# Top-2 expert routing in a two-layer kernel: how the threshold, the slots and the token lists are computed

## The reference

```python
def _L1_ffn_ref(x, router_w, wg, wu, wd):
    E, K, CF = 8, 2, 1.25
    xf = x.reshape(-1, D)                      # N = 4096 tokens
    capacity = max(1, int(CF * N / E))         # 640
    probs = jax.nn.softmax(xf @ router_w.T, axis=-1)
    topw, topi = jax.lax.top_k(probs, K)
    topw = topw / (topw.sum(-1, keepdims=True) + 1e-06)
    fe, fw, ft = topi.reshape(-1), topw.reshape(-1), jnp.repeat(jnp.arange(N), K)
    order = jnp.lexsort((-fw, fe))             # by expert, heaviest first
    se, sw, st = fe[order], fw[order], ft[order]
    rank = jnp.arange(N * K) - starts[se]
    keep = rank < capacity                     # an expert keeps its 640 heaviest
    disp = ...                                 # the kept tokens, [E, 640, D]
    eo = (silu(disp @ wg) * (disp @ wu)) @ wd  # per expert
    out = zeros.at[st].add(eo[...] * (sw * keep)[:, None])
```

## Time and profile before

| | us |
|---|---|
| median of 3 runs | 3220.86 (3217.69 to 3222.49) |
| the profiled execution | 3225.83 |
| its span, from the first instruction to the last | 3224.0 |

### The profile page before, as it was taken

How to read it: one execution, slowest core, us unless ns; L and a number is a source line. 1 busy time by engine, 2 the same in 40 slices (tenths; PEclk the granted TensorE clock), 3 DMA queues, 4 the chain that set the end, 5 groups by cost and what they waited for, 6 DMA issues and landing times. The chain is left out here.

```text
span 3224.0 us, 46683 instructions
## 1 busy us (share of the span) xinstructions
PE 2902.0 (90%) x16106; PEld 1942.3 (60%) x16106; DVE 2127.2 (66%) x4522; ACT 1732.5 (54%) x3308; POOL 1750.2 (54%) x1540
## 2 busy tenths in 40 slices
PE   7999999999999999979954859999999999999176
PEld 6995555565555556558843845656656566565075
DVE  5667777777777777646766336677676766766642
ACT  5666767777676776756731424444444444443032
POOL 0006988889898888831102825454454544444066
PEclk9999999999999999989976979999999999999578
DMA  2004434343343433300011444444444444432034
GB/s 95 1 21 99 100 80 100 82 98 87 90 94 89 93 87 86 74 30 15 21 63 39 78 96 99 102 102 93 112 92 97 102 102 102 104 88 60 26 77 77
DMA packets 182988, 254.00 MB, mean 79 GB/s; under 512 B 35904, under 2 KB 75584, under 8 KB 182208
## 3 DMA queue, kind: packets, MB, share of 16 engines
q1 hardware_dynamic: 168672, 240.19, 31.6%
q0 software_dynamic: 14080, 10.82, 2.5%
HBM read 33.44 MB, written 16.67 MB: 16 GB/s over the span
## 5 line engine op out<-in xcount | busy, mean ns | idle before, releaser
L1766 POOL TENSOR_TENSOR arena<-arena 128x512 f32<-128x512 f32 x1152 | 1444.8, 1283 | 719.6 <-ACT arena L1137 695.8
L794 PE MATMUL psum<-stack 96*128 96x512 f32 (+4 forms) x4096 | 1240.9, 433 | 31.3 <-ACT arena L1137 11.5
L1137 ACT ACTIVATE arena<-psum 128x512 f32<-128x512 f32 x1536 | 854.5, 598 | 507.0 <-PE psum L794 471.0
L1396 DVE TENSOR_REDUCE top<-psum 128x1 f32<-128x512 f32 x1536 | 978.2, 676 | 137.5 <-PE psum L794 130.7
L794 PEld LDWEIGHTS psum<-stack 96*128 96x128 f32 (+4 forms) x4096 | 715.2, 191 | 428.4 <-issue 206.1
L824 PE MATMUL psum<-arena,values 128*32 128x512 f32 (+1 forms) x3072 | 493.6, 598 | 0.5
L824 PEld LDWEIGHTS psum<-arena,values 128*32 128x32 f32 (+1 forms) x3072 | 132.1, 119 | 271.6 <-issue 230.5
L1735 POOL TENSOR_SCALAR rstd<-mv 128x4 f32<-128x4 f32 x56 | 12.8, 229 | 488.0 <-DVE mv L1258 486.6
L782 PE MATMUL psum<-xT,wqkv 128*128 128x512 f32 x512 | 272.1, 613 | 4.2 <-DVE X L1458 3.3
L1427 DVE RECIPROCAL psum<-psum 128x128 f32<-128x128 f32 x256 | 236.4, 943 | 9.2 <-PE psum L856 9.2
L694 PE MATMUL psum<-stack 128*128 128x512 f32 x768 | 214.2, 415 | 19.8 <-DVE stack L1295 19.8
(11 more groups left out here) (155 smaller groups left out, 3105.1 us busy)
## 6 DMA issues: line engine op xcount, KB each, us to landing
stack<-halves SPq DMA_DIRECT2D x768, 128.0 KB, 2.3
stack<-halves SPq DMA_DIRECT2D x384, 256.0 KB, 4.7
tokens<-xn SPq DMA_DIRECT2D x16, 256.0 KB, 2.5
sums<-X SPq DMA_DIRECT2D x16, 256.0 KB, 2.8
arena<-in_wg SPq DMA_DIRECT2D x16, 256.0 KB, 3.0
arena<-in_wu SPq DMA_DIRECT2D x16, 256.0 KB, 3.4
arena<-in_wd SPq DMA_DIRECT2D x16, 256.0 KB
wqkv<-in_w_qkv SPq DMA_DIRECT2D x2, 1536.0 KB, 9.1
```

The costliest lines, as they stand in the source:

```text
L794: ins = T_.matmul(bk, st[0:k, side, slot + h, cols], st[0:k, 1 - side, slot + h, :], start=r == 0, stop=r == len(PARTS[l]) - 1)
L1137: S_.activation(prob[l][tile % N_PROB][:, h, :], psum[:, bank[key], :], ACT.Exp, scale=scale).then_inc(released[bank[key]], 1)
L1396: give(V_.reduce_max(top[i][:, j:j + 1], psum[:, bank[key], :], AX.X), key)
L1766: ins = G_.tensor_tensor(to[:, h, :], old[:, h, :], prob[l][tile % N_PROB][:, h, :], ALU.add)
```

## The change

The search keeps two values ready for each bit: `met` is the next candidate if the count is reached, `missed` if it is not. Both are computed from `cand` alone, behind the count. The matrix now holds 4.0 in place of 1.0, and a second product, with the constant column `share`, is added in the same bank, so that a reached count gives a large number and an unreached one a negative number (or zero). One operation with two per-partition scalars, min and then max, then picks the next candidate. The threshold is the last candidate.

The slots are computed as [expert, tile] instead of [tile, expert], with bf16 flags. A running sum over the tiles is one `tensor_tensor_scan` for each kind of flag (`going_on` is 0 at an expert's first tile). PE adds up the parts: flags in the partitions at or after, negative and divided by 128, the running sum divided by 128, and the expert's first slot, all as bf16 products into one bank. A slot number is thus held divided by 128, plus 1. A third sum tells which ties fit. As two experts of a token have different codes, one maximum and one sum over the experts give both, in place of the ranks, and `R` is gone.

The one-hot tiles have the tiles innermost, and every operand of the comparisons is bf16. ACT makes the bf16 tables (`make_tables`) ahead of its first weight split, and the half of `row_hot` with the partition's number.

```diff
 def search(s):                                  # PE
+    pe.wait_ge(tables, TABLES * (s + 1))
     for i in range(TOP_BIT + 1):
-        pe.wait_ge(searching, s * (TOP_BIT + 3) + i + 1)
         bk, done = place(("reach", s, TOP_BIT - i))
-        T_.matmul(bk[:, 0:1], same_bf16, cnt, start=True, stop=True).then_inc(done, 1)
+        T_.matmul(bk[:, 0:1], same_bf16, share_bf16, start=True, stop=False)
+        pe.wait_ge(searching, s * (TOP_BIT + 2) + i + 1)
+        T_.matmul(bk[:, 0:1], same_bf16, cnt, start=False, stop=True).then_inc(done, 1)
...
 def positions(s):                               # PE
-    T_.matmul(bk, before, flat, start=True, stop=True).then_inc(done, 1)
-    T_.matmul(bk, ones[:, :], flat, start=True, stop=True).then_inc(done, 1)
+    def slots_before(bk, kind, offset):
+        T_.matmul(bk[:, 0:n], below_bf16, flags[:, kind], start=True, stop=False)
+        T_.matmul(bk[:, 0:n], all_bf16, upto[:, kind], start=False, stop=False)
+        ins = T_.matmul(bk[:, 0:n], all_bf16, offset, start=False, stop=kind == 0)
+        if kind:
+            ins = T_.matmul(bk[:, 0:n], all_bf16, upto[:, 0, :, TILES - 1:TILES].to_broadcast(wide), ...)
+    for kind in range(2):
+        pe.wait_ge(flagged, 2 * s + kind + 1)
+        slots_before(bk, kind, slot0_bf16.unsqueeze(2).to_broadcast(wide)).then_inc(done, 1)
+    slots_before(bk, 1, minus_tiles.unsqueeze(2).to_broadcast(wide)).then_inc(done, 1)
+    pe.wait_ge(row_parts, s + 1)
     for j in range(n_all):
-        ins = T_.matmul(bk[:, 0:2 * SLOT_ROWS], within_hot[j // step % 2][:, j % step, :],
-                        row_hot[:, j, :, :].rearrange("p x r -> p (x r)"), ...)
+        ins = T_.matmul(bk[:, 0:2 * SLOT_ROWS].rearrange("p (x r) -> p x r", x=2),
+                        within_hot[j // STEP % 2][:, :, j % STEP],
+                        row_hot[:, :, :, j], start=j == 0, stop=j == n_all - 1)
...
+make_tables()                                   # ACT
 split_weights(0)
+act.wait_ge(rows_hot, s + 1)
+S_.activation(row_hot[:, 0, :, :], slot_hot, ACT.Copy, scale=row_number).then_inc(row_parts, 1)
...
 def search(s):                                  # DVE, one bit
     tick(V_.tensor_scalar(reach, weight_t, cand, None, ALU.is_ge, ALU.add, accum_out=cnt), searching)
+    tick(V_.tensor_scalar(bits(met), bits(cand), below_it, None, ALU.bitwise_or))
+    a = tick(V_.tensor_scalar(bits(missed), bits(cand), (1 << bit) | below_it, None, ALU.bitwise_xor))
     dve.wait_ge(*written(key))
-    a = give(V_.tensor_scalar(bits(bit_step), psum[:, bank[key], 0:1], float(CAP), float(1 << bit), ...), key)
-    a = tick(V_.scalar_tensor_tensor(out=bits(cand), in0=bits(bit_step), scalar=1 << (bit - 1), in1=bits(thr), ...))
-    t0 = tick(V_.tensor_tensor(bits(thr), bits(thr), bits(bit_step), ALU.bitwise_or))
+    a = give(V_.tensor_scalar(cand, psum[:, bank[key], 0:1], met, missed, ALU.min, ALU.max), key)
...
 def positions(s):                               # DVE, the lists
+    for i in range(blocks):
+        a = tick(V_.tensor_tensor(slot_hot[:, :, j], numbers[:, 1:1 + SLOT_ROWS, :],
+                                  rows_j.unsqueeze(1).to_broadcast(part), ALU.is_equal), ...)
+    tick(V_.tensor_tensor(row_hot[:, 1, :, :], slot_hot,
+                          tile_number.unsqueeze(1).to_broadcast([P, SLOT_ROWS, n_all]), ALU.mult))
+    for i in range(blocks):
+        tick(V_.tensor_tensor(within_hot[i % 2], numbers,
+                              within_flat[:, i * STEP:(i + 1) * STEP].unsqueeze(1).to_broadcast(part),
+                              ALU.is_equal), hot)
```

More of the change, by code:

```diff
@@ L328, in experts1 @@
         self.once(self.other, ("threshold", s))
-        self.once(self.products, ("inside", s))
-        self.once(self.products, ("totals", s))
+        for kind in range(2):
+            self.once(self.products, ("place", s, kind))
+        self.once(self.products, ("room", s))
         self.once(self.other, ("tokens", s))
@@ L920, in positions @@
+                for kind in range(2):
+                    pe.wait_ge(flagged, 2 * s + kind + 1)
+                    bk, done = place(("place", s, kind))
+                    slots_before(bk, kind, slot0_bf16.unsqueeze(2).to_broadcast(wide)).then_inc(done, 1)
+                bk, done = place(("room", s))
+                slots_before(bk, 1, minus_tiles.unsqueeze(2).to_broadcast(wide)).then_inc(done, 1)
                 bk, done = place(("tokens", s))
-                n_all, step = 2 * TILES, 16
+                n_all = 2 * TILES
@@ L1573, in positions, with count_up @@
+                w = W.rearrange("p t e -> p e t")
                 over, tied = flags[:, 0], flags[:, 1]
+                def count_up(kind):
+                    tick(V_.tensor_tensor_scan(upto[:, kind].rearrange(flat), going_on.rearrange(flat),
+                                               flags[:, kind].rearrange(flat), 0.0, ALU.mult, ALU.add), flagged)
                 dve.wait_ge(*written(key))
-                tick(V_.tensor_tensor(over, W, thr_b, ALU.is_gt))
-                a = give(V_.tensor_tensor(tied, W, thr_b, ALU.is_equal), key)
+                a = tick(V_.tensor_tensor(over, w, thr_b, ALU.is_gt))
@@ L1594, in positions @@
-                upto, pos = scan[i], scan[1 - i]
-                key = ("inside", s)
+                count_up(0)
+                a = give(V_.tensor_tensor(tied, w, thr_b, ALU.is_equal), key)
                 dve.wait_ge(*a)
-                dve.wait_ge(*written(key))
-                a = give(V_.tensor_copy(pos.rearrange(flat), psum[:, bank[key], 0:n_flags]), key)
+                a = tick(V_.scalar_tensor_tensor(out=tied, in0=w, scalar=0.0, in1=tied, op0=ALU.is_gt, op1=ALU.mult))
                 dve.wait_ge(*a)
-                a = tick(V_.tensor_tensor(pos[:, :, 1:, :], pos[:, :, 1:, :], upto[:, :, :TILES - 1, :], ALU.add))
@@ L1601, in positions, with result @@
-                all_over = upto[:, 0, TILES - 1:TILES, :].to_broadcast(wide)
-                pos_o, pos_t = pos[:, 0], pos[:, 1]
+                count_up(1)
+                def result(key):
+                    dve.wait_ge(*written(key))
+                    return psum[:, bank[key], 0:TILES * EXPERTS].rearrange("p (e t) -> p e t", e=EXPERTS)
+                c = give(V_.tensor_tensor(code, result(("place", s, 0)), over, ALU.mult), ("place", s, 0))
+                a = give(V_.scalar_tensor_tensor(out=fits, in0=result(("room", s)), scalar=0.0, in1=tied,
+                                                 op0=ALU.is_lt, op1=ALU.mult), ("room", s))
@@ L1603, in positions @@
                 dve.wait_ge(*a)
-                a = tick(V_.tensor_tensor(pos_t, pos_t, all_over, ALU.add))
+                a = give(V_.tensor_tensor(placed, result(("place", s, 1)), fits, ALU.mult), ("place", s, 1))
+                dve.wait_ge(*c)
                 dve.wait_ge(*a)
-                a = tick(V_.scalar_tensor_tensor(out=tied, in0=pos_t, scalar=float(CAP), in1=tied,
-                                                 op0=ALU.is_lt, op1=ALU.mult))
-                m0, m1, m2 = tmp
+                a = tick(V_.tensor_tensor(code, code, placed, ALU.add))
@@ L1619, in positions @@
[L1619 to L1628 removed]
+                a = tick(V_.tensor_copy(within, bits(idx)))
@@ new lines, in positions @@
+                blocks = n_all // STEP
+                dve.wait_ge(tables, TABLES * (s + 1))
+                for i in range(blocks):
+                    j = slice(i * STEP, (i + 1) * STEP)
+                    part = [P, SLOT_ROWS, STEP]
+                    rows_j = slot_row.rearrange("p k t -> p (k t)")[:, j]
+                    a = tick(V_.tensor_tensor(slot_hot[:, :, j], numbers[:, 1:1 + SLOT_ROWS, :],
+                                              rows_j.unsqueeze(1).to_broadcast(part), ALU.is_equal),
+                             rows_hot if i == blocks - 1 else step_done)
```

205 lines of the change are left out of this document (89 added, 116 removed).

## The result

| | before | after |
|---|---|---|
| median of 4 runs each, us | 3221.47 (3217.69 to 3222.49) | 3193.77 (3192.32 to 3195.90) |
| the profiled execution, us | 3225.83 | 3192.57 |
| chain from copy to last count, first call, us | 73.13 | 59.24 |

The changed kernel takes 0.9912 of the time before (95% interval 0.9901 to 0.9924). That is 27.7 us less, some 14 a call. The forecast was 3177 (3166 to 3192), 43.4 less, so the direction is right and the time lies outside the range. A repeat on another chip gave 25.7 us less (0.9921, 0.9908 to 0.9935).

A forecast was written before the change was run, and what follows sets the result against it. The chain over DVE and PE was taken as the bound, no engine. Gains of 0.4 + 2.7 + 11.2 + 7.4 = 21.7 a call, 43.4 in all, gave 3177 us from 3220.86, range 3166 to 3192.

The forecast's parts named there:

- What bounds the kernel: Second MoE's routing: no engine is the bound but the chain over DVE and PE, 73.1 and 73.3 us in two calls.
- Ahead of the search: Copy of the weights to first count: memsets into DVE's idle time, cast to ACT, 0.85 to 0.46 us, gain 0.4 a call.
- The search: Loop over 30 bits: a bit takes 1.07 us instead of 1.159, gain 2.7 us a call.
- That just fits: In each bit, `met` and `missed` take 0.27 us within the 0.28 that DVE sat idle for PE.
- The stated low end, 0.6: Bit loop's smallest gain a call, in us, if `met` and `missed` don't overlap (0.35 in the 0.28).
- The slots: Flags to row comparison, L1575 to L1647: 19.8 us becomes 8.55, gain 11.2 a call, ends 12.5 and 8.2.
- The lists: Row comparison to last count, L1647 to L1669: 16.95 us becomes 9.53, gain 7.4 a call, better end 8.5.
- PE's blocks of 1.23: One-hot products near the chain's end: four PE blocks of 1.23 us each run from 4.40 to 9.50.
- one rival (9.4): PE's operands with large steps: a product costs twice, lists end at 14.2, 9.4 in both calls, 3187; chance 0.20.
- The pairs don't come: DVE's bf16 comparisons run one element a cycle: gain 1.1 instead of 7.4, 3190; chance 0.12.
- Slower than before: PE's strided reads cost far more, 0.42 a product cancels the gain; at four cycles a read 3255; chance 0.03.
- Better: Pick's scalars nearly free and PE's clock up in the lists: 4 us more a call, 3169; chance 0.10.

The follow-up runs named there:

- combined: Changed kernel with one-scalar pick, its second wait on a memset, weights and columns in groups of two tiles, PE's room products earlier: 3178.32 us, ratio 0.9868.

## Why the prediction was wrong in its size

- **What bounds the kernel: right.** The chain was the bound before and is now. Its gain in the two calls, 28.0 us, is the gain of the kernel, 27.7. In the first call GpSimd's wait fell by 13.9, and the chain by 13.9.
- **Ahead of the search: right.** 0.39 for 0.4. The tables on ACT were done at 1657.3, and the first product that reads them starts at 1658.9.
- **The search: the failed step is "That just fits".** It asked whether `met` and `missed` end before the pick can start, and they do: `missed` ends 0.21 us after `met` starts. It didn't ask what a second wait does to the pick. With the late wait last it starts 0.07 us later after PE's product than L1558 did, and 30 times 0.07 is 2.2 of the 2.8 missing. The same kernel with the waits swapped takes 1.087 a bit, near the 1.07 that was forecast. The rest, 0.017 a bit, is mostly in the pick and its hand-over, which take 0.31 to 0.32 where the sum had 0.30. The stated low end, 0.6, didn't reach zero, since it had only one way to be late.
- **The slots: right in their parts.** Scan 0.69 as taken; strided operations 0.58 to 0.61 for 0.55; reductions 0.58 for 0.5 and 0.6. Four and four products follow the second scan, and the text counted four and three: 1.98 from the end of that scan to L1645, for 1.75. In all 8.99 in place of 8.55.
- **The lists: the failed step is "PE's blocks of 1.23".** It took the price of a product from the earlier trace rows, where the columns lie side by side, for a product whose columns lie 128 bytes apart. A block took 2.55. DVE's side was right: the bf16 comparisons run in pairs of elements, 1.22 us for 1.14 (and for the 1.224 that the prediction quotes), row comparisons 0.42 each, the product 1.49, ACT's half 2.43 and hidden. The forecast had the right mechanism as a rival with the right size, a product that costs twice and lists of 14.2, and gave it 0.20. What spoke against it, that at 1.2 GHz a column is asked for only each 0.83 ns, carried no number for a strided read. No row of the trace had one, and the rule that the prediction itself cited spoke for the rival.
- **The range.** Its upper end took in the rivals singly. The time came from one rival (9.4) and the search (5.6) together, which makes 3192, and 2 x 0.44 from the slots make it 3192.9.
- **The rivals.** "The pairs don't come" fell (1.22 us). "Slower than before" by strided reads needed 0.42 a product; it was 0.150. "Better" had scalars nearly free; they cost 0.06 each.
- The gain that was forecast, 43.4, is there: combined reached 44.5 with the same idea, once the columns lay close and the pick started on time. But it also has a pick with one scalar less (0.06 a bit, 3.6 us in both calls) and another order of PE's products (0.4 a call), so this does not make the forecast's working right.

## What to carry to other kernels

When two engines hand each other one small operation in a loop, look at the start of the waiting instruction, not only at whether its inputs are ready: issue the wait that ends last first, so that the instruction itself holds it, and where the order can't be chosen, let a filler operation take the early wait. When an operation's layout is turned for one engine's sake, price the other engine's read of it, and look for a layout that serves both: two tiles innermost kept DVE's pairs and gave PE back its columns. A step with an unpriced read between "free" and "twice" belongs in the range together with the other open prices, not instead of them.

## What the runs showed of the hardware

- Two waits on an instruction: with the one that ends last in the last place, the start is 0.07 us later on DVE (0.30 against 0.23 behind the product) and 0.06 on PE's load (0.20 against 0.14). In the other order the second wait is free. The second wait issued sits in an instruction of its own ahead of the work, and the delay is the way from that instruction to the next. The Trainium skill ("VectorE: DVE Perf Modes", Rules for kernel authors) advises to keep the count of chained operations down, and not to mind the semaphores. This loop is an exception: one more operation of 0.06 us, which took a wait over, saved 0.07 a bit.
- A scalar read per partition adds 0.06 us to a one-element DVE operation (0.158, 0.219, 0.277 with none, one and two; the middle one has a second tensor of one element instead).
- At the clock level of 0.50, one bf16 product of 128 by 80 follows the other after 0.149 us with its columns 128 bytes apart, 0.079 to 0.081 with 8, and 0.067 with 4 or with them side by side. Its weights may lie 32 bytes apart for 0.002 to 0.009.
- A `tensor_tensor_scan` over 256 bf16 elements takes 0.69 us, against 0.58 to 0.61 for the strided flag operations around it. Reductions of 256 fp32 elements take 0.57 to 0.58 with a step of 32 elements, against 0.42 without a step. The flag operations rose from 0.42 to these 0.6 too, but there the output turned to bf16 at the same time.
- A comparison of 2048 bf16 elements takes 1.22 us with 16, 4 or 2 tiles innermost, where its other operand is repeated over the rest.
